# Loading TensorE's weight-address registers two at a time instead of eight at a time in a mixture-of-experts loop

## The chip, the cores and the metric

The kernel runs on one NeuronCore of a Trainium2 chip. The metric is the device time of one execution in microseconds (us), the median of several runs. The core has five engines that run side by side and wait for one another through semaphores: TensorE (PE, matrix products; its weight loads are shown apart as PEld), VectorE (DVE), ScalarE (ACT), GpSimd (POOL) and SyncE (SP), which here only starts transfers. Each engine has a sequencer that reads its instructions in order; instructions that only the sequencer handles (register arithmetic, loads into registers, semaphore waits) are shown in the profile with a q behind the engine's name.

## What is computed

The reference is one transformer layer on x of shape 4 x 1024 x 128: causal attention with 16 heads, then a mixture of 8 experts of which each token takes 2, plus a shared expert. The part that the change touches is the experts:

```python
logits = xn @ gate_w.T
probs = jax.nn.softmax(logits, axis=-1)
tk_probs, tk_idx = jax.lax.top_k(probs, TOP_K)
...
out = _swiglu(xf, sWg, sWu, sWd)
for e in range(NUM_EXPERTS):
    out = out + w[:, e:e + 1] * _swiglu(xf, Wg[e], Wu[e], Wd[e])
```

where `_swiglu(x, wg, wu, wd)` is `silu(x @ wg) * (x @ wu) @ wd`, with 128 inputs, 256 inner columns and 128 outputs.

## The kernel before

The kernel first projects and stores queries and keys, then runs attention (until about 635 us of the span), then the experts. The 8192 pairs of token and expert are sorted by expert into rows of a tensor in HBM, `sorted_rows`, and padded so that each tile of 128 rows belongs to one expert. There are `TILES` = 72 tiles, worked off as `NP` = 36 pairs; the loop variable of the pair is `q`.

Which expert a tile belongs to is known only at run time. It is written as an offset into the weights to `w_at`, one int32 for each tile, in on-chip memory. PE reads it from there into its own registers with `pe.load` (the instruction TENSOR_LOAD, line 1721, in `load_regs(a, n)`: n registers, for tiles a to a+n-1). There are `BATCH` = 24 registers, and tile k uses register k % 24. `expert_at(k)` (line 1770) turns such a register into the address that the weight operands of `tile_gate_up` and `tile_down` use. SP has 24 registers of its own for the rows of `sorted_rows` and loads them 24 at a time at line 1262, and 8 for the padding at line 1248.

The tile table comes in two parts. The first 24 offsets (`EARLY_TILES`) are loaded into registers ahead of the loop, 8 at a time. The other 48 are loaded in the loop: from `q` = `LATE_FROM` = 9 on, `AHEAD` = 3 pairs ahead of their use, behind a wait for the transfers that write the table (`tiles_in`).

One turn of the loop on PE, for pair q, holds in this order:

- `tile_gate_up(q, 0)`: three matmuls against 512 columns for the gate and up weights (lines 1786 to 1788; the operands are split in two parts so that three passes give the product),
- `turn_h(q - 1)`: four transposes of the pair before (line 1794), which wait for DVE's product `tile_h(q - 1)` (line 1587),
- `tile_gate_up(q, 1)`, then `turn_rows(q + 2)`: two transposes of the rows that come two pairs later (line 1776),
- `tile_down(q - 1)`: eight matmuls of the down projection (line 1805), which wait for DVE's copy `keep_hT(q - 1)` (line 1594),
- on some turns, `load_regs`.

Beside it ACT does `tile_silu(q)` (line 1383), `keep_hi(q + 2)` (line 1377) and `keep_y(q - 1)` (line 1391). DVE does, each turn, `destination(q)` (lines 1578 and 1581), `keep_hT(q - 1)` (line 1594), `tile_h(q)` (line 1587), pieces of the final sum and its norm from q = 23 on (a hand-written table, `PIECES`: adds at line 1433, statistics at lines 1424, 1449 and 1452), and `keep_lo(q + 2)` (line 1570). POOL scatters the results (line 1309). SP fetches rows, nine pairs deep. Each engine runs its instructions in the order in which the code writes them; no scheduler reorders them.

The profile's names for buffers are those of the memory that they reuse: `k_space` on line 1805 is the transposed hidden tile, `q_space` on line 1587 the hidden tile, `expT` the fetched rows.

Of the kernel before, what the change touches and what calls it, by code (L numbers as in the profile page):

```python
# [219 lines left out]
def block_kernel(nc, x_d, wq_d, wqs_d, bq_d, wk_d, wks_d, bk_d, wkv_d, bkv_d, wv_d, bv_d, wo_d, bo_d,  # L220
# [13 lines left out]
    with ExitStack() as top:  # L234
# [778 lines left out]
        with ExitStack() as two:  # L1013
# [149 lines left out]
            AHEAD, LATE_FROM = 3, EARLY_TILES // 2 - 3  # L1163
            B_XT, B_HT, B_Y = (0, 1), 7, 6
            NP = TILES // 2
# [516 lines left out]
            def tensor_behind(pe, item):  # L1682
# [37 lines left out]
                def load_regs(a, n):  # L1720
                    pe.load(regs[a % BATCH:a % BATCH + n], w_at[0:1, a:a + n])
# [50 lines left out]
                def turn_rows(q):  # L1772
                    pe.wait_ge(xt_in[q % TILE_RING], DMA * 2 * (q // TILE_RING + 1))
                    wait(pe, t_lo_ok, q - 1)
                    for i in range(2):
                        last = nc.tensor.transpose(ps[:, B_XT[q % 2], P * i:P * (i + 1)], xt[:, q % TILE_RING, i, 0:E], identf[:])
                    last.then_inc(xt_turned, 1)

                def tile_gate_up(q, i):
                    at = expert_at(2 * q + i)  # L1780
                    if i == 0:
                        pe.wait_ge(t_lo_ok, q + 1)
                        wait(pe, h_ok, q - 1)
                    out = ps[:, 2 + 2 * (q % 2) + i]
                    hi, lo = t_hi[:, q % 2, P * i:P * (i + 1)], t_lo[:, q % 2, P * i:P * (i + 1)]
                    nc.tensor.matmul(out, hi, wide_hi[:, bass.ds(at, 2 * INTER)], start=True, stop=False)  # L1786
                    nc.tensor.matmul(out, hi, wide_lo[:, bass.ds(at, 2 * INTER)], start=False, stop=False)  # L1787
                    nc.tensor.matmul(out, lo, wide_hi[:, bass.ds(at, 2 * INTER)], start=False, stop=True).then_inc(gu_ok, 1)  # L1788

                def turn_h(q):  # L1790
                    pe.wait_ge(h_ok, q + 1)
                    wait(pe, hT_ok, q)
                    for i in range(4):
                        last = nc.tensor.transpose(ps[:, B_HT, P * i:P * (i + 1)], hu[:, q % 2, P * i:P * (i + 1)],  # L1794
                                                   identf[:])
                    last.then_inc(h_turned, 1)

                def tile_down(q):
                    pe.wait_ge(hT_ok, q + 1)
                    wait(pe, y_kept, 2 * q)  # L1800
                    for i in range(2):
                        at = expert_at(2 * q + i)
                        out = ps[:, B_Y, P * i:P * (i + 1)]
                        for f in range(2):
                            last = nc.tensor.matmul(out, hT[:, q % 2, INTER * i + P * f:INTER * i + P * (f + 1)],  # L1805
                                                    wide_down[:, bass.ds(at + P * f, P)], start=f == 0, stop=f == 1)
                    last.then_inc(y_made, 1)
# [7 lines left out]
                for q in range(NP):  # L1815
                    tile_gate_up(q, 0)
                    if q > 0:
                        turn_h(q - 1)
                    tile_gate_up(q, 1)
                    if q + 2 < NP:  # L1820
                        turn_rows(q + 2)
                    if q > 0:
                        tile_down(q - 1)
                    if q == LATE_FROM:
                        pe.wait_ge(tiles_in, 4 * DMA)
                    if q >= LATE_FROM and (q - LATE_FROM) % 4 == 0 and q + AHEAD < NP:
                        load_regs(2 * (q + AHEAD), 8)
                turn_h(NP - 1)
                gate_up(FRONT, 0)
                tile_down(NP - 1)  # L1830
# [380 lines left out]
            def _(pe):  # L2211
# [116 lines left out]
                for s in range(NS - LAG, NS):  # L2328
                    for part in range(2):
                        product(G - 1, s, part)  # L2330
                tensor_behind(pe, item)


# [44 lines left out]
```

## Time and profile before

| what | value |
| --- | --- |
| median of 3 runs | 819.85 us (818.8 to 823.23) |
| the profiled execution's own time | 819.85 us |
| span from its first to its last instruction | 818.1 us |
| PE busy | 735.1 us, 90% of the span |
| PE weight loads busy | 352.7 us, 43% |
| DVE busy | 628.3 us, 77% |
| ACT busy | 510.6 us, 62% |
| POOL busy | 337.0 us, 41% |
| TensorE clock granted, mean | 0.96 of full speed |

The profiled execution took what the median run took; 1.75 us of it lie outside the span. The rows are read as follows. The chain of waits follows the work that ended last back to the beginning. The timeline has instructions in order of time, with the idle time of the engine just before them in brackets and what ended it. The view of one line of the code gives its instructions' durations in ns as smallest, median and largest.

### The profile page before, as it was taken

What the parts mean: (1) busy time and instruction counts of PE and PEld (TensorE: products, weight loads), DVE (VectorE), ACT (ScalarE), POOL (GpSimd) and SP (SyncE); (2) the same over time, 40 slices, a digit from 0 to 9 for tenths busy, and PEclk for the clock granted to TensorE, in tenths of its full rate; (3) what the DMA queues carried; (4) which work ended last, traced back from release to release, by engine and by line L of the source; (5) the groups of instructions that cost most, each with busy time, mean ns of one, the idle gap of its engine ahead of it and who ended that gap; (6) DMA issues with size and microseconds to landing.
All of it is one profiled execution on the core that took longest, in us unless ns stands there. A gap on an engine that the chain in (4) does not pass through costs nothing.

```text
span 818.1 us, 17480 instructions
## 1 busy us (share of the span) xinstructions
PE 735.1 (90%) x5616; PEld 352.7 (43%) x5616; DVE 628.3 (77%) x1969; ACT 510.6 (62%) x1045; POOL 337.0 (41%) x518
## 2 busy tenths in 40 slices
PE   5788689999999999989999999999998989999991
PEld 2343123333334333433433433433333867787771
DVE  5979878988886897887788688689653557656886
ACT  3655146666766778666686776677888734444553
POOL 3666221232221323215554223464336447655662
PEclk9978579999999999999999999999999999999997
DMA  6459552413614315224153241431230423435423
GB/s 164 140 153 187 137 151 49 69 29 41 105 46 73 60 36 106 48 36 87 40 101 72 64 68 27 95 69 53 67 98 31 102 83 110 134 82 153 132 92 119
DMA packets 78529, 71.79 MB, mean 88 GB/s; under 512 B 27154, under 2 KB 58547, under 8 KB 78259
## 3 DMA queue, kind: packets, MB, share of 16 engines
q1 hardware_dynamic: 69528, 59.32, 33.0%
q0 software_dynamic: 4352, 8.99, 3.5%
q10 hardware_dynamic: 4562, 2.40, 1.1%
q8 instruction: 46, 0.75, 0.4%
q14 instruction: 41, 0.34, 0.1%
HBM read 44.24 MB, written 23.94 MB: 83 GB/s over the span
## 4 chain that ended last, share of the span: by engine, by line
PE 59%; DVE 12%; issue 7%; ACT 6%; DMA 1%; POOL 1%; POOLq 0%; SPq 0%; DVEq 0%; ACTq 0%
PE ps L2292 15%; PE ps L2319 14%; PE ps L306 11%; DVE x_in L317 5%; ACT expT L2026 4%; PE ps L1805 4%; PE ps L1786 2%; PE ps L1788 2%; PE ps L1787 2%; PE ps L1794 2%; PE ps L1714 1%; PE ps L2269 1%; ACT rows L752 1%; PE ps L977 1%; PE ps L993 1%
## 5 line engine op out<-in xcount | busy, mean ns | idle before, releaser
L2026 ACT ACTIVATE expT<-ps 128x512 f32<-128x512 f32 (+1 forms) x640 | 333.0, 553 | 148.5 <-PE ps L2319 141.4
L317 DVE CUSTOM_DVE_ANT_0 x_in<-ps,mask 128x1024 bf16<-128x1024 f32 (+7 forms) x512 | 364.2, 754 | 56.9 <-PE ps L306 53.2
L2319 PE MATMUL ps<-q_space,k_space 96*128 96x512 bf16 (+3 forms) x768 | 223.2, 333 | 8.7 <-ACT expT L2026 5.1
L306 PE MATMUL ps<-k_space,q_space 96*128 96x512 bf16 (+3 forms) x768 | 196.9, 342 | 19.3 <-DVE mx L317 15.5
L2292 PE MATMUL ps<-expT,vr 128*9 128x256 f32 (+1 forms) x2560 | 178.3, 360 | 0.9 <-POOL expT L1980 0.9
L1980 POOL TENSOR_SCALAR_AFFINE_SELECT expT<-expT 128x512 f32<-128x512 f32 x128 | 79.7, 635 | 194.7 <-ACT expT L2026 194.2
L2319 PEld LDWEIGHTS ps<-q_space,k_space 96*128 96x128 bf16 x768 | 61.9, 98 | 159.9 <-ACT expT L2026 103.6
L306 PEld LDWEIGHTS ps<-k_space,q_space 96*128 96x128 bf16 x768 | 63.9, 99 | 83.2 <-DVE mx L317 48.7
L742 POOL DMA_INDIRECT sorted_rows<-rows,places x64 | 64.0, 1000 | 58.2 <-ACT expT L2026 33.8
L1309 POOL DMA_INDIRECT expert_rows<-expT,tile_to x72 | 70.0, 972 | 38.4 <-ACT expT L1391 21.0
L2292 PEld LDWEIGHTS ps<-expT,vr 128*9 128x9 f32 x2560 | 41.3, 88 | 92.2 <-issue 47.6
L1933 POOL TENSOR_SCALAR negs<-mx 128x16 bf16<-128x16 f32 x32 | 8.4, 263 | 108.2 <-DVE mx L317 96.6
L1383 ACT ACTIVATE q_space<-ps 128x512 f32<-128x512 f32 x36 | 21.5, 597 | 44.1 <-PE ps L1788 44.1
L1805 PE MATMUL ps<-w_gu,k_space 128*128 x288 | 41.4, 287 | 4.1 <-DVE k_space L1594 3.8
L317 DVE DVE_READ_ACCUMULATOR2_ANT mx<- 128x1 f32 x512 | 42.4, 83 | 0.0
L1587 DVE TENSOR_TENSOR q_space<-q_space,ps 128x512 f32<-128x512 f32 x36 | 24.7, 687 | 20.5 <-ACT q_space L1383 20.5
L1805 PEld LDWEIGHTS ps<-w_gu,k_space 128*128 128x128 f32 x288 | 34.8, 191 | 11.8 <-issue 11.8
L1786 PE MATMUL ps<-w_hi,rows_hi 128*128 x72 | 34.4, 478 | 2.3 <-DVE q_space L1587 1.3
L1594 DVE COPY k_space<-ps 128x512 f32<-128x512 f32 x36 | 24.9, 691 | 14.2 <-PE ps L1794 14.0
L1391 ACT ACTIVATE expT<-ps,expT 128x128 f32<-128x128 f32 x72 | 22.5, 364 | 20.5 <-PE ps L1805 20.5
L1788 PE MATMUL ps<-w_hi,rows_lo 128*128 x72 | 28.4, 395 | 0.0
L1787 PE MATMUL ps<-w_lo,rows_hi 128*128 x72 | 28.2, 392 | 0.0
(239 smaller groups left out, 916.2 us busy)
## 6 DMA issues: line engine op xcount, KB each, us to landing
q_space<-q_parts SPq DMA_DIRECT2D x48, 192.0 KB
expT<-sorted_rows SPq DMA_DIRECT2D x72, 65.0 KB, 1.9
k_space<-k_parts SPq DMA_DIRECT2D x32, 128.0 KB
q_parts<-parts SPq DMA_DIRECT2D x24, 128.0 KB, 2.4
k_parts<-parts SPq DMA_DIRECT2D x24, 128.0 KB, 3.0
k_space<-k_parts SPq DMA_DIRECT2D x16, 192.0 KB
v_ones<-v_st SPq DMA_DIRECT2D x8, 288.0 KB, 3.4
vr<-v_ones SPq DMA_DIRECT2D x16, 144.0 KB
```

The source lines that it names most:

```text
L306: last = nc.tensor.matmul(psw[:, at + lo:at + hi], qr[:, g % RING, hh, qi * P:(qi + 1) * P], kr[:, g % RING, hh, lo:hi], start=True, stop= ...
L317: last = nc.vector.tensor_tensor_reduce(out=unread[:, odd, col:col + width], in0=psw[:, 2 * CT * odd + col:2 * CT * odd + col + width], in ...
L742: nc.gpsimd.indirect_dma_start(out=xs_d, out_offset=bass.IndirectOffsetOnAxis(ap=pos[:, q, k, c * NT + t:c * NT + t + 1], axis=0), in_=xs[ ...
L1309: nc.gpsimd.indirect_dma_start(out=y_d, out_offset=bass.IndirectOffsetOnAxis(ap=to[:, r, i:i + 1], axis=0), in_=yt[:, r, i], in_offset=Non ...
L1786: nc.tensor.matmul(out, hi, wide_hi[:, bass.ds(at, 2 * INTER)], start=True, stop=False)
L1787: nc.tensor.matmul(out, hi, wide_lo[:, bass.ds(at, 2 * INTER)], start=False, stop=False)
L1788: nc.tensor.matmul(out, lo, wide_hi[:, bass.ds(at, 2 * INTER)], start=False, stop=True).then_inc(gu_ok, 1)
L1805: last = nc.tensor.matmul(out, hT[:, q % 2, INTER * i + P * f:INTER * i + P * (f + 1)], wide_down[:, bass.ds(at + P * f, P)], start=f == 0 ...
L1980: nc.gpsimd.affine_select(out=tile, in_=tile, compare_op=ALU.is_ge, fill=0.0, base=0, pattern=[[0, GH], [1, P]], channel_multiplier=-1).th ...
L2026: act.activation(expT[:, (NS * g + s) % PTN, hh, 0:width], ps[:, B_S + hh % 2, 0:width], ACT.Exp, scale=SCALE).then_inc(exp_ok, 1)
L2292: last = nc.tensor.matmul(ps[32 * hh:32 * hh + VW, B_O + half, at:at + n], vr[:, g % RING, kt, hh * VW:(hh + 1) * VW], expT[:, (NS * g + s ...
L2319: last = nc.tensor.matmul(ps[:, B_S + hh % 2, col:col + m], kr[:, g % RING, hh, kt * P:(kt + 1) * P], qr[:, g % RING, hh, q0:q0 + m], star ...
```

## The change

The loads of the loop are cut up. Before, on turns q = 9, 13, 17, 21, 25 and 29, one instruction loads 8 registers. After, on each turn from q = 9 to q = 32, one instruction loads 2 registers. The same 48 values go to the same 48 places in the ring of registers; those of pair q + 3 are loaded on turn q in both or, before, up to three turns earlier. The wait for `tiles_in` stays on turn 9. The loads ahead of the loop stay 3 of 8 registers.

```diff
                     if q == LATE_FROM:
                         pe.wait_ge(tiles_in, 4 * DMA)
-                    if q >= LATE_FROM and (q - LATE_FROM) % 4 == 0 and q + AHEAD < NP:
-                        load_regs(2 * (q + AHEAD), 8)
+                    if LATE_FROM <= q < NP - AHEAD:
+                        load_regs(2 * (q + AHEAD), 2)
```

The first place is on PE between turn 10 and turn 11, of the kernel before. The rows at L1805 are the end of `tile_down(9)`, those from L1786 on the start of `tile_gate_up(11, 0)`; ISA and REGISTER_ALU are the register arithmetic of the weights' address.

```order
L1770 ISA
L1805 MATMUL ps<-w_gu,k_space 128x128
L1805 ISA
L1805 MATMUL ps<-w_gu,k_space 128x128
L1786 ISA
L1786 MATMUL ps<-w_hi,rows_hi 128x512
L1787 REGISTER_ALU
L1787 MATMUL ps<-w_lo,rows_hi 128x512
L1788 MATMUL ps<-w_hi,rows_lo 128x512
```

The same place on PE in the changed kernel.

```order
L1770 ISA
L1805 MATMUL ps<-w_gu,k_space 128x128
L1805 ISA
L1805 MATMUL ps<-w_gu,k_space 128x128
L1721 TENSOR_LOAD w_at
L1786 ISA
L1786 MATMUL ps<-w_hi,rows_hi 128x512
L1787 REGISTER_ALU
L1787 MATMUL ps<-w_lo,rows_hi 128x512
L1788 MATMUL ps<-w_hi,rows_lo 128x512
```

One load has come between the last matmul of a turn and the address arithmetic of the next. It has done so at 18 turns (10 to 12, 14 to 16, 18 to 20, 22 to 24, 26 to 28, 30 to 32); at the six turns that had a load it stands where it stood. PE's program is 18 rows longer, and nothing else in it differs.

The second place is on DVE in turn 28, one of the turns with statistics. Its rows are the same in both kernels: `tile_h(28)`, the statistics of one chunk, `keep_lo(30)`, `destination(29)`, and `keep_hT(28)`, for which PE's `tile_down(28)` waits.

```order
L1587 TENSOR_TENSOR q_space<-q_space,ps 128x512
L1424 BN_STATS out_stats<-q_space 128x6 x4
L1449 BN_AGGR out_mean_var<-out_stats 128x2 x4
L1452 TENSOR_SCALAR out_var_eps<-out_mean_var 128x4
L1570 TENSOR_TENSOR rows_lo<-ps,rows_hi 128x256
L1578 SCALAR_TENSOR_TENSOR dump_rows<-expT,tab 128x2
L1581 TENSOR_TENSOR tile_to<-dump_rows,expT 128x2
L1594 COPY k_space<-ps 128x512
```

Nothing has moved on DVE, ACT, POOL or SP.

## Rows read from the trace of the kernel before

**Rows 1.** The page, chain that ended last, by engine.
```profile
PE 59%; DVE 12%; issue 7%; ACT 6%; DMA 1%; POOL 1%; POOLq 0%; SPq 0%; DVEq 0%; ACTq 0%
```

**Rows 2.** Busy time by stretch, turns 9 to 21; the columns are in the row.
```profile
core 0: us, PE busy (x) PEld busy (x) DVE busy (x) ACT busy (x) POOL busy (x), PEclk, DMA share, GB/s
...
701.12:740.49 39.37, 38.71 (x241) 31.58 (x240) 23.33 (x60) 17.98 (x49) 23.11 (x25) 1.00 0.33 91
```

**Rows 3.** Waits, 701.1 to 792 us: waiter, releaser, us in total, times, longest.
```profile
PE ps L1805 <- DVE k_space L1594: 2.9, 5, 0.8
PEld ps L1786 <- issue: 2.6, 6, 0.5
```

**Rows 4.** Timeline of PEld, first weight load of each `tile_down`: start, us [idle before].
```profile
701.12 0.97 PEld L1805 LDWEIGHTS ps<-w_gu,k_space 128*128 128x128 f32 x8 [0.19 <-issue]
704.77 0.97 PEld L1805 LDWEIGHTS ps<-w_gu,k_space 128*128 128x128 f32 x8 [0.20 <-issue]
707.92 0.97 PEld L1805 LDWEIGHTS ps<-w_gu,k_space 128*128 128x128 f32 x8 [0.19 <-issue]
...
714.25 0.97 PEld L1805 LDWEIGHTS ps<-w_gu,k_space 128*128 128x128 f32 x8 [0.19 <-issue]
717.91 0.97 PEld L1805 LDWEIGHTS ps<-w_gu,k_space 128*128 128x128 f32 x8 [0.18 <-issue]
...
727.39 0.97 PEld L1805 LDWEIGHTS ps<-w_gu,k_space 128*128 128x128 f32 x8 [0.19 <-issue]
731.01 0.97 PEld L1805 LDWEIGHTS ps<-w_gu,k_space 128*128 128x128 f32 x8 [0.19 <-issue]
...
740.49 0.97 PEld L1805 LDWEIGHTS ps<-w_gu,k_space 128*128 128x128 f32 x8 [0.20 <-issue]
744.25 0.97 PEld L1805 LDWEIGHTS ps<-w_gu,k_space 128*128 128x128 f32 x8 [0.19 <-issue]
747.41 0.97 PEld L1805 LDWEIGHTS ps<-w_gu,k_space 128*128 128x128 f32 x8 [0.18 <-issue]
750.73 0.97 PEld L1805 LDWEIGHTS ps<-w_gu,k_space 128*128 128x128 f32 x8 [0.34 <-issue]
753.89 0.97 PEld L1805 LDWEIGHTS ps<-w_gu,k_space 128*128 128x128 f32 x8 [0.19 <-issue]
757.81 0.97 PEld L1805 LDWEIGHTS ps<-w_gu,k_space 128*128 128x128 f32 x8 [0.43 <-issue]
760.97 0.97 PEld L1805 LDWEIGHTS ps<-w_gu,k_space 128*128 128x128 f32 x8 [0.19 <-issue]
764.18 0.97 PEld L1805 LDWEIGHTS ps<-w_gu,k_space 128*128 128x128 f32 x8 [0.24 <-issue]
768.05 0.97 PEld L1805 LDWEIGHTS ps<-w_gu,k_space 128*128 128x128 f32 x8 [0.91 <-issue]
771.69 0.97 PEld L1805 LDWEIGHTS ps<-w_gu,k_space 128*128 128x128 f32 x8 [0.19 <-issue]
775.49 0.97 PEld L1805 LDWEIGHTS ps<-w_gu,k_space 128*128 128x128 f32 x8 [0.83 <-issue]
778.77 0.97 PEld L1805 LDWEIGHTS ps<-w_gu,k_space 128*128 128x128 f32 x8 [0.33 <-issue]
781.94 0.97 PEld L1805 LDWEIGHTS ps<-w_gu,k_space 128*128 128x128 f32 x8 [0.19 <-issue]
```

**Rows 5.** Timeline of all engines, after turn 9's load and in turn 29.
```profile
702.50 0.19 PEld L1786 LDWEIGHTS ps<-w_hi,rows_hi 128*128 128x128 f32 x1 [0.41 <-issue]
...
768.06 1.15 PE L1805 MATMUL ps<-w_gu,k_space 128*128 x8 [0.68 <-DVE k_space L1594]
```

**Rows 6.** PE's register loads by line, whole span, then 740 to 742 us: min/median/max ns.
```profile
L1721 PEldq TENSOR_LOAD <-w_at x9: 589/595/992, 638.4 to 768.5; - x9
...
L1721 PEldq TENSOR_LOAD <-w_at x1: 667/667/667, 741.0 to 741.0; - x1
```

**Rows 7.** SP's register loads by line: 8 registers (L1248), 24 registers (L1262), ns.
```profile
L1248 SPq TENSOR_LOAD <-pad_at x1: 539/539/539, 661.7 to 661.7; - x1
...
L1262 SPq TENSOR_LOAD <-row_at x2: 1527/1534/1542, 694.1 to 728.5; - x2
```

## The prediction, made before the changed kernel was run

> **What bounds the kernel now.** I read the chain of waits first: 59% of it is PE, the next engine has 12% [rows 1]. The change touches only the expert loop's turns 9 to 32, so that stretch decides. In turns 9 to 21 PE is busy 38.71 of 39.37 us, and DVE, the next, 23.33 [rows 2]: there PE's order is the time. From turn 23 on DVE has the final sum beside its usual work, and PE now and then waits for DVE's copy, five times for 2.9 us in all [rows 3].
>
> The beat of the loop is read off the first weight load of each `tile_down` [rows 4]. The row at 701.12 is turn 9, then each row is the next turn; the third row is turn 11, 714.25 turn 13, 727.39 turn 17, and from 740.49, turn 21, every turn stands there up to 781.94, turn 33. A plain turn lasts 3.16 us (757.81 to 760.97, and 744.25 to 747.41). A turn with a load of 8 registers lasts 3.65 (turn 9), 3.66 (turn 13), 3.62 (turn 17), 3.76 (turn 21) and 3.64 (turn 29). So such a load costs 0.49, 0.50, 0.46, 0.60 and 0.48 us of PE's time. The sixth, turn 25, is read below. The same stalls show as PE's weight load at line 1786 idle with nothing to wait for, 2.6 us in 6 times [rows 3], 0.41 us in the one of turn 9 [rows 5].
>
> The load itself takes 0.59 us (0.589 smallest, 0.595 median of nine; 0.667 on turn 21) [rows 6]. It costs 0.49 and not 0.59 because the sequencer runs a little ahead of the array: the eight matmuls of `tile_down` are still being worked off when the load starts. **About 0.10 us of a load are hidden by this cover, the rest stalls PE.**
>
> **The change part by part.** It removes six loads of 8 registers and puts in 24 loads of 2. How many registers are loaded stays the same, 48. All hangs on what a load of 2 takes, and the trace of before has none on any engine.
>
> *The price of a load of 2.* The nearest rows are SP's: 8 registers took 0.539 us, 24 registers 1.534 (two of them, within 1%) [rows 7]. That is 1.534 - 0.539 = 0.995 us for 16 more registers, 0.062 each, and a straight line through both leaves 0.04 us for a load of none. So time goes nearly as the number of registers. On PE, six registers fewer make 0.59 - 6 x 0.062 = 0.22 us. The lower bound is pure proportion, 0.59 x 2/8 = 0.15; the upper one is that two cost what eight do, 0.59, since no row lies below 8 and a fixed part could hide behind it. I take 0.22, the line through the rows that exist; both ends are kept for the range.
>
> The Trainium skill speaks for either end. "DMA: Bandwidth & Descriptors", section "Latency and other measured facts", gives `tensor_load` a floor of about 600 ns, which a compiler is said to spread over four unrolled iterations. By it 24 loads would cost as much each as the six did, and the change would be the wrong way round; PE's 0.589 fits it, SP's 0.539 is a little under it. "Runtime: NRT & Kernel Launch", section "Instruction fetch mechanics", says that such loads cost about 200 ns for each register even in bulk. That is for HBM, and in size it is far from the 0.062 here, but its form is the line above. The two can't both hold for 2 registers.
>
> *The stall of a load of 2.* 0.22 less the cover of 0.10 is 0.12 us where PE is the bound. The cover is the same at every turn, since what precedes the load is the same eight matmuls.
>
> *Where the 24 loads fall.* Where PE waits for DVE anyway, a load before that wait is hidden. PEld's idle time before `tile_down` is 0.19 us on a plain turn; what it is above that is the slack that the turn before it has to give [rows 4]: 0.15 for turn 23 (row 750.73), 0.24 for turn 25 (757.81), 0.05 for turn 27 (764.18), 0.72 for turn 28 (768.05), 0.64 for turn 30 (775.49), 0.14 for turn 31 (778.77). In these turns DVE's run from `tile_h` through sum or statistics, `keep_lo` and `destination` to `keep_hT` ends last. It starts from the gate and up products of the turn's own pair, which stand ahead of that turn's load, so the load can't push it. In turn 28 PE itself sits idle 0.68 us for that copy [rows 5].
>
> Sum, in us, new stalls less old:
> - turns 9 to 20: 12 x 0.12 = 1.44, less 0.49 + 0.50 + 0.46 = 1.45: **-0.01**
> - turns 21 to 24: three at 0.12 and turn 23's within its 0.15, 0.36, less 0.60: **-0.24**
> - turns 25 to 28: turn 26 0.12, turn 27 0.12 - 0.05 = 0.07, turns 25 and 28 hidden; the old load of turn 25 gives nothing back, since its turn of 3.92 us ended with a wait for DVE that only grows if the load shrinks: **+0.19**
> - turns 29 to 32: turns 29 and 32 0.12 each, 30 and 31 hidden, 0.24, less 0.48: **-0.24**
>
> Together -0.3 us. Behind turn 32 the last pairs and the tail (scatter, fetch back, norm, store) follow from PE's last `tile_down`, so a shift of the loop reaches the end undiminished. ACT, DVE, POOL and SP issue what they issued; their rings wait for PE or are ahead of it. The wait for the second part of the table stays on turn 9 and is as early or late as before. Registers arrive at least three turns ahead of use, so nothing waits for a late load. Against the profiled execution's 819.85, which is the median too, this makes **819.5 us**.
>
> **The rivals.** *A fixed price for each load.* The 18 added loads, on PE's sequencer between `tile_down` and the next `tile_gate_up`, then stall 0.49 each in an open turn. By the same four groups: 12 x 0.49 - 1.45 = 4.43; 3 x 0.49 + 0.34 - 0.60 = 1.21; 0.49 + 0.44 = 0.93; 2 x 0.49 + 0.35 - 0.48 = 0.85; together +7.4, **827.3 us**. It is slower by more than 0.5% from the point where a load of 2 takes about 0.43 us (a stall of 0.33: 2.51 + 0.57 + 0.61 + 0.37 = 4.1). For it: there is no row below 8 registers, and a read has some latency whatever its size. Against it: 24 registers took 2.8 times what 8 took, and a fixed part big enough would have shown as an intercept, which is 0.04.
> This is also where the floor in the skill's DMA page, named above, would put the time.
>
> *A part of it fixed.* PE's load is 0.05 us longer than SP's for the same 8, so PE may have a fixed part of its own, or registers may be read in groups. With 0.40 us for a load of 2, a stall of 0.30: 2.15 + 0.45 + 0.55 + 0.28 = +3.4, **823.3 us**, still within 0.5%.
>
> *Wholly hidden.* If a load of 2 takes 0.10 to 0.15 us, the stalls are 0 to 0.05, and the old ones are gained: at 0, -1.45 - 0.60 - 0.48 = -2.5, **817.3 us**; at 0.05, -1.6, 818.2. For it: pure proportion. Against it: both engines show a little more than proportion. No further gain is to be had, as the six loads cost no more than that.
>
> **How the numbers follow.** The line through SP's rows, 0.17 to 0.27 us a load: 0.65. Partly fixed, up to 0.43: 0.11. Fixed, over 0.43: 0.15. Hidden or nearly, under 0.17: 0.09. The range takes in the hidden end and the partly fixed one and about 1 us on the outer side of each for the runs' own scatter (lowest and median of before are 1.05 apart): 816.8 to 824.5; it leaves out most of the fixed case. A measurement of this kernel can tell about 0.5%, 4.1 us, from no change. Faster by that needs more than the loads cost: 0.04, for scatter alone. Slower is the fixed case and a little of the partly fixed: 0.17. Within 0.5%: 0.79.
>
> **What would show it.** In the changed trace line 1721 has 27 loads, 24 of them short. At 0.20 to 0.25 us each the price is right; at 0.59 the rival is. Turns 10 to 12 should last 3.28 us, all alike, not 3.16 and not 3.65; turns 25, 28 and 30 should stay at 3.92, 3.87 and 3.80. PE's weight load at line 1786 should be idle a short time at 24 turns instead of 0.4 us at six. Wrong would also be a cover that differs from 0.10: since 24 loads are each reduced by it and six were, 0.05 more or less of it moves the sum by up to 1 us (19 of them are not hidden).

## The result, and the profile after

The changed kernel takes 828.0 us (median of 6 runs, 826.9 to 829.81), the kernel before 820.08 beside it (6 runs). The ratio is 1.0096, with a 95% interval of 1.0074 to 1.0118: slower by 1%, outside the range of the prediction and on the side of its first rival, which had 827.3.

The profiled execution has a span of 826.0 us, 7.9 more than before. The page still has PE at the head of the chain that ended last (before: [rows 1]).

```profile
PE 57%; DVE 13%; ACT 7%; issue 7%; POOL 1%; DMA 1%; POOLq 0%; SPq 0%; DVEq 0%; ACTq 0%
```

The view of line 1721 has the register loads: all 27 of the span, then the 13 of turns 9 to 21, then one on turn 31, as smallest, median and largest duration in ns (before: [rows 6]).

```profile
L1721 PEldq TENSOR_LOAD <-w_at x27: 536/561/1286, 638.6 to 786.8; - x27
...
L1721 PEldq TENSOR_LOAD <-w_at x13: 538/556/670, 701.8 to 745.5; - x13
...
L1721 PEldq TENSOR_LOAD <-w_at x1: 1286/1286/1286, 782.5 to 782.5; - x1
```

A load of 2 registers in the loop takes 0.56 us in the median (0.54 to 0.67 but for the one on turn 31), hardly less than the 0.59 of one with 8; the prediction had 0.22. The timeline of PEld, at the first weight load of each `tile_down` as in [rows 4], has turns 9 to 12 and the borders of the groups of turns: 701.39 is turn 9, 744.99 turn 21, 759.52 turn 25, 763.44 turn 26, 774.68 turn 29, 789.97 turn 33.

```profile
701.39 0.97 PEld L1805 LDWEIGHTS ps<-w_gu,k_space 128*128 128x128 f32 x8 [0.19 <-issue]
704.99 0.97 PEld L1805 LDWEIGHTS ps<-w_gu,k_space 128*128 128x128 f32 x8 [0.20 <-issue]
708.69 0.97 PEld L1805 LDWEIGHTS ps<-w_gu,k_space 128*128 128x128 f32 x8 [0.20 <-issue]
712.28 0.97 PEld L1805 LDWEIGHTS ps<-w_gu,k_space 128*128 128x128 f32 x8 [0.19 <-issue]
...
744.99 0.97 PEld L1805 LDWEIGHTS ps<-w_gu,k_space 128*128 128x128 f32 x8 [0.19 <-issue]
...
759.52 0.97 PEld L1805 LDWEIGHTS ps<-w_gu,k_space 128*128 128x128 f32 x8 [0.19 <-issue]
763.44 0.97 PEld L1805 LDWEIGHTS ps<-w_gu,k_space 128*128 128x128 f32 x8 [0.47 <-issue]
...
774.68 0.97 PEld L1805 LDWEIGHTS ps<-w_gu,k_space 128*128 128x128 f32 x8 [0.53 <-issue]
...
789.97 0.97 PEld L1805 LDWEIGHTS ps<-w_gu,k_space 128*128 128x128 f32 x8 [0.19 <-issue]
```

Turns 9 to 11 last 3.60, 3.70 and 3.59 us, where before one in four lasted 3.65 and the others 3.16. Set against [rows 4], group by group:

| turns | before, us | after, us | difference | prediction | fixed-price rival |
| --- | --- | --- | --- | --- | --- |
| 9 to 20 | 39.37 | 43.60 | +4.23 | -0.01 | +4.43 |
| 21 to 24 | 13.40 | 14.53 | +1.13 | -0.24 | +1.21 |
| 25 to 28 | 14.16 | 15.16 | +1.00 | +0.19 | +0.93 |
| 29 to 32 | 13.89 | 15.29 | +1.40 | -0.24 | +0.85 |

The four make 7.76 of the 7.9 us; turn 9 begins 0.27 us later, and what follows turn 32 is 0.1 to 0.2 us shorter. The waits of the loop (701.3 to 800 us; waiter, releaser, us in total, times, longest) have the stalls in one row. Where [rows 3] had 2.6 us in 6 times, it is now 10.1 in 24.

```profile
PEld ps L1786 <- issue: 10.1, 24, 1.1
```

### The profile page after: what moved, and what is told of

The parts are those of the page before. It is cut to its first block, busy times and chain, and to the rows that moved or that the text cites. A ratio compares the mean times of both kernels' runs of the same rounds, so it can differ in the third digit from the quotient of the medians.

```text
span 826.0 us, 17498 instructions
## 1 busy us (share of the span) xinstructions
PE 735.7 (89%) x5616; PEld 352.5 (43%) x5616; DVE 628.5 (76%) x1969; ACT 510.7 (62%) x1045; POOL 337.4 (41%) x518
## 4 chain that ended last, share of the span: by engine, by line
PE 57%; DVE 13%; ACT 7%; issue 7%; POOL 1%; DMA 1%; POOLq 0%; SPq 0%; DVEq 0%; ACTq 0%
PE ps L2292 15%; PE ps L2319 14%; PE ps L306 11%; DVE x_in L317 5%; ACT expT L2026 4%; PE ps L1786 3%; DVE q_space L1587 2%; PE ps L1788 2%; PE ps L1787 2%; PE ps L1805 2%; ACT q_space L1383 2%; PE ps L1794 2%; PE ps L1714 1%; PE ps L2269 1%; ACT rows L752 1%
## 5 line engine op out<-in xcount | busy, mean ns | idle before, releaser
L1805 PE MATMUL ps<-w_gu,k_space 128*128 x288 | 41.4, 287 | 3.0 <-DVE k_space L1594 2.9
L1786 PE MATMUL ps<-w_hi,rows_hi 128*128 x72 | 34.7, 482 | 6.5 <-DVE q_space L1587 4.3
L1805 PEld LDWEIGHTS ps<-w_gu,k_space 128*128 128x128 f32 x288 | 34.8, 191 | 10.6 <-issue 10.6
```

## The experiments

The chips of the experiments are slower than the one of the result (the medians of the kernel before lie between 833 and 838 us there). The loop has the same turns of 3.16 and 3.65; turn 9 begins 12 to 16 us later, at 713 to 718 us. All their profiles show the granted clock at half of full speed for 14 to 21 us between 672 and 703 us, ahead of turn 9, which the two profiles of the result don't show: the mean from 670 to 700 us is 0.77 in e1_ladder and 1.00 in the kernel before. Some of the chips scatter by several us. So each time is given as a ratio to the kernel before in the same set of runs, and what a turn or a load lasts is read from the profiles.

### Are the loads in the loop worth what the turns say?

e3_none leaves the six loads out, and with them the right weights for the tiles from 24 on.

```diff
-                    if q >= LATE_FROM and (q - LATE_FROM) % 4 == 0 and q + AHEAD < NP:
-                        load_regs(2 * (q + AHEAD), 8)
```

> The kernel before without the six loads in the loop. It leaves out their effect: the tiles from 24 on are multiplied with the weights of other experts' offsets that the registers still hold, so the output differs; the instructions and their shapes are the same. It measures what all loads in the loop cost together. By the stalls read from the turns (0.49, 0.50, 0.46, 0.60, 0.48, and turn 25's hidden) the time is 2.5 us less than before: 817.5, all plain turns at 3.16 us and turn 25 still 3.9, held by DVE. A rival: the turns with a load only gather waits that would be there without it, then less than 1 us is gained.

The timed runs fell into two groups, about 832 to 836 and 841 to 845; the ratio is 1.0008 (0.9954 to 1.0062) and doesn't settle whether 2.5 us are gained. The profile does, for the open turns: 717.54, 720.70, 723.86 are turns 9, 10 and 11, and every turn from 9 to 22 lasts 3.16 to 3.18 us. Those 14 turns take 44.31 us, and 46.25 in the profile of e1_ladder, which turned out to be the kernel before on the same chip (see below). The 1.94 us between them are what the four loads of these turns cost by the length of the turns. So the stalls come from the loads.

```profile
717.54 0.97 PEld L1805 LDWEIGHTS ps<-w_gu,k_space 128*128 128x128 f32 x8 [0.21 <-issue]
720.70 0.97 PEld L1805 LDWEIGHTS ps<-w_gu,k_space 128*128 128x128 f32 x8 [0.20 <-issue]
723.86 0.97 PEld L1805 LDWEIGHTS ps<-w_gu,k_space 128*128 128x128 f32 x8 [0.19 <-issue]
```

### Number of loads or number of registers?

e2_each8 was to have 24 loads of 8.

```diff
-                    if q >= LATE_FROM and (q - LATE_FROM) % 4 == 0 and q + AHEAD < NP:
-                        load_regs(2 * (q + AHEAD), 8)
+                    if LATE_FROM <= q < NP - AHEAD:
+                        load_regs(8 * ((q + AHEAD) // 4), 8)
```

> 24 loads at the same turns as in the changed kernel, but of 8 registers each: the aligned group of 8 that holds those of the pair three turns ahead, so most loads rewrite values that are there. If the number of loads sets the price (A), a load takes 0.59 us and not 0.55, the turns last 3.65 and the time is that of the changed kernel or up to 1 us more: 828 to 829. If the number of registers had a share of 0.06 us each beyond the fixed part (B in the loop), six more registers would cost 0.37 us at each of some 20 open turns: 835.

The built kernel has only 12 of the 24: a load whose registers are all loaded again before one of them is read is left out. What remains is two loads on neighbouring turns for each group of 8. The ratio is 1.0046 (1.0005 to 1.0088). The view of line 1721 has 15 loads with those ahead of the loop, and the first two turns with a load, 11 and 12, last 3.74 and 3.66 us.

```profile
L1721 PEldq TENSOR_LOAD <-w_at x15: 587/594/1010, 640.3 to 798.3; - x15
...
722.55 0.97 PEld L1805 LDWEIGHTS ps<-w_gu,k_space 128*128 128x128 f32 x8 [0.19 <-issue]
726.29 0.97 PEld L1805 LDWEIGHTS ps<-w_gu,k_space 128*128 128x128 f32 x8 [0.19 <-issue]
729.95 0.97 PEld L1805 LDWEIGHTS ps<-w_gu,k_space 128*128 128x128 f32 x8 [0.19 <-issue]
```

So six more loads of 8 cost about what six stalls do (6 x 0.49 = 2.9 us, 0.4%). That fits a price for each load, but also one for what a load holds. e6_four goes the other way, with 12 loads of 4.

```diff
-                    if q >= LATE_FROM and (q - LATE_FROM) % 4 == 0 and q + AHEAD < NP:
-                        load_regs(2 * (q + AHEAD), 8)
+                    if q >= LATE_FROM and (q - LATE_FROM) % 2 == 0 and q + AHEAD < NP:
+                        load_regs(2 * (q + AHEAD), 4)
```

> One part of the change: 12 loads of 4 registers, on turns 9, 11, ... 31. Theory A (the price hangs on the number of loads; 0.55 us each, 0.45 of it stall in an open turn): six more loads than before, of which those on turns 11, 15, 19, 23, 27 and 31 are new; at 0.45 and with 0.15, 0.05 and 0.14 hidden on the last three, 2.4 us, less 0.04 saved on each old one: +2.2 us, a ratio of 1.003. Theory B (the line of the prediction, 0.34 us a load of 4, 0.24 of stall): 12 x 0.24 less the old 2.5, about 0.

The ratio is 0.9991 (0.9975 to 1.0007), no difference. A load of 4 takes 0.335 us in the median, and turns 9 and 11 last 3.37 and 3.41 us, 0.21 and 0.25 more than a plain one.

```profile
L1721 PEldq TENSOR_LOAD <-w_at x15: 331/335/972, 639.2 to 790.2; - x15
...
715.03 0.97 PEld L1805 LDWEIGHTS ps<-w_gu,k_space 128*128 128x128 f32 x8 [0.19 <-issue]
718.40 0.97 PEld L1805 LDWEIGHTS ps<-w_gu,k_space 128*128 128x128 f32 x8 [0.20 <-issue]
721.55 0.97 PEld L1805 LDWEIGHTS ps<-w_gu,k_space 128*128 128x128 f32 x8 [0.19 <-issue]
```

Theory A, a fixed price for a load, falls: 4 registers cost 0.34, which is what the line of the prediction gives, and 2 registers cost 0.56. The smaller load is the dearer one.

### The price by size

e1_ladder was to measure the price by itself.

> The kernel before with loads added behind its last work: PE, behind its last matmul, loads 1, 2, 4, 8, 9, 12, 16 and 24 registers, three times each; SP does the same behind the last stores. It measures the disputed price by itself. Theory A (a fixed latency that covers up to 8 registers, then more for each further one): 1, 2, 4 and 8 registers within 0.05 us of each other at 0.53 to 0.60 us, 24 at about 1.5; 9, 12 and 16 tell whether the rise is a step for each group of 8 (9 as long as 16, about 1.0) or a slope (9 about 0.6, 16 about 1.05). Theory B (a line in the number, as the prediction took; the loop's loads of 2 were long for another reason, such as traffic in the loop): 1 register 0.1, 2 registers 0.17 to 0.22, 4 registers 0.3, 8 registers 0.55 us. PE's loads end before the last transfers, so the span changes only by SP's 24 loads at the end, some 18 us by A.

The added loads are not in the built kernel, for the reason given above, so it shows only the kernel before on that chip: turn 9 at 3.64 us, its load at 0.593. e7_sizes cuts the loads unevenly, with all values used.

```diff
-                load_regs(0, 8)
-                load_regs(8, 8)
+                load_regs(8, 16)
-                load_regs(16, 8)
+                load_regs(0, 1)
+                load_regs(1, 1)
+                load_regs(2, 2)
+                load_regs(4, 4)
...
+                SIZES = {9: (24, 12), 15: (36, 12), 21: (48, 9), 25: (57, 15)}
```

> The price by size, in loads whose registers are all used. Ahead of the loop 16 registers in one load and then 1, 1, 2 and 4; in the loop 12 on turn 9, 12 on turn 15, 9 on turn 21, 15 on turn 25, instead of six of 8. Theory A, flat up to 8: 1, 2 and 4 take 0.53 to 0.57 us each. If further registers come in groups of 8: 9, 12, 15 and 16 all take about the same, near 1.1. If they come at the 0.062 us each of SP's rows: 9 at 0.65, 12 at 0.85, 15 at 1.0, 16 at 1.1. Theory B: 1 at 0.15, 2 at 0.22, 4 at 0.34, 16 at 1.1. (A ladder of loads behind the kernel's end had been built for e1_ladder, but loads whose values nobody uses are left out when the kernel is built, so that run shows only the kernel before.)

The view of the load line, in narrow windows: 1 register, 4, 12 on turn 9, 9 on turn 21, 15 on turn 25.

```profile
L1723 PEldq TENSOR_LOAD <-w_at x1: 315/315/315, 662.5 to 662.5; - x1
...
L1723 PEldq TENSOR_LOAD <-w_at x1: 339/339/339, 664.0 to 664.0; - x1
...
L1723 PEldq TENSOR_LOAD <-w_at x1: 883/883/883, 713.9 to 713.9; - x1
...
L1723 PEldq TENSOR_LOAD <-w_at x1: 857/857/857, 753.6 to 753.6; - x1
...
L1723 PEldq TENSOR_LOAD <-w_at x1: 3717/3717/3717, 768.0 to 768.0; - x1
```

1 and 4 cost nearly the same, and 9 costs as much as the first load of 12; the second 12, on turn 15, took 1.04. The 2 between the 1 and the 4 took 0.66, the 16 took 1.29. The load of 15 seems out of any line, and its turn lasts 8.01 us; the next run explains it. The law that came out of this (law F): registers are read four at a time, what is left over one at a time, and each read takes about 0.25 us. e9_sizes2 tests it with other sizes and with starts that are not divisible by four.

```diff
+                SIZES = {9: [(24, 7)], 10: [(31, 1)], 12: [(32, 3)], 13: [(35, 5)], 14: [(40, 6)], 15: [(46, 2)],
+                         17: [(48, 4)], 18: [(52, 4)], 20: [(56, 8)], 24: [(64, 2)], 26: [(66, 4)], 27: [(70, 2)]}
...
```

> More sizes, to test a law formed from e7_sizes, e6_four and the changed kernel: 1 register 0.31 us, 2 0.54 (0.66 once), 4 0.33, 8 0.59, 9 0.86, 12 0.88, 16 1.29. Law F: registers are read four at a time, about 0.27 us a read on PE, and what is left over of a multiple of four is read one at a time at the same 0.27, with 0.05 once; so n costs 0.05 + 0.27 x (n div 4 + n mod 4). It gives 3 registers 0.86, 5 0.59, 6 0.86, 7 1.13, and 4 0.32. Ahead of the loop stand 3 (tile 0), 5 (3), 6 (8), 2 (14), 1 (16), 4 (17), 3 (21); in the loop 7 on turn 9, 1 on 10, 3 on 12, 5 on 13, 6 on 14, 2 on 15, 4 on 17 and 18, 8 on 20, 2 on 24, 4 (from 66) on 26, 2 on 27. Law G: only a start divisible by four is read in fours; then the 4 from tile 17 and the 4 from 66 take 1.13. Theory B (a line) would have 3 at 0.28, 6 at 0.47, 7 at 0.53: all below 8's 0.59.

The loads of turns 9, 10, 12, 13, 14, 15, 17 and 26, in this order: 7, 1, 3, 5 (from tile 35), 6, 2, 4 (from 48) and 4 (from 66).

```profile
L1724 PEldq TENSOR_LOAD <-w_at x1: 1092/1092/1092, 717.0 to 717.0; - x1
...
L1724 PEldq TENSOR_LOAD <-w_at x1: 308/308/308, 721.3 to 721.3; - x1
...
L1724 PEldq TENSOR_LOAD <-w_at x1: 801/801/801, 727.8 to 727.8; - x1
...
L1724 PEldq TENSOR_LOAD <-w_at x1: 1362/1362/1362, 731.6 to 731.6; - x1
...
L1724 PEldq TENSOR_LOAD <-w_at x1: 860/860/860, 736.0 to 736.0; - x1
...
L1724 PEldq TENSOR_LOAD <-w_at x1: 534/534/534, 740.0 to 740.0; - x1
...
L1724 PEldq TENSOR_LOAD <-w_at x1: 348/348/348, 746.8 to 746.8; - x1
...
L1724 PEldq TENSOR_LOAD <-w_at x1: 1014/1014/1014, 777.7 to 777.7; - x1
```

3 registers cost more than 8 did, 7 more still, as law F has it. The last two rows are both loads of 4; the one that starts at tile 66 takes three times as long. And the 5 from tile 35 cost as much as five reads, though 36 to 39 could have been one. Law G holds: only a load that starts at a place divisible by four is read in fours. Of the loads ahead of the loop, 5 from tile 3 took 1.24, 6 from tile 8 took 0.85, 2 from tile 14 took 0.55 and 1 took 0.31, as the law has them; 4 from tile 17 (1.27) and 3 from tile 21 (1.13) took 0.25 and 0.33 more than the 4 from tile 66 and the 3 from tile 32, and why is not known.

Law G also accounts for the 3.72 us in e7_sizes. Its 15 registers start at tile 57, which is not divisible by four, so they are 15 reads: at 0.25 each about 3.8 us. The turn of 8.01 us holds more than this load: behind it, from 771.90 to 775.51 us, the mean granted clock is 0.55.

### Twice the registers on the same turns

e10_four_each has the changed kernel's turns, with 4 registers on 22 of them.

```diff
-                        load_regs(2 * (q + AHEAD), 2)
+                        load_regs(2 * (q + AHEAD), 2 if (q + AHEAD) % 12 == 11 else 4)
```

> The changed kernel with 22 of its 24 loads made twice as long: 4 registers, for the next pair but three and the one behind it, where it has 2 (turns 20 and 32, where four would run past the end of the ring or the table, keep 2). Half of the loads start at a tile divisible by four. Law F: each such load is 0.33 us and not 0.54, its stall 0.24, turns 10 to 12 last 3.40, and the loop costs 22 x 0.21 = 4.6 us less than the changed kernel at most, about 4 with those that are hidden: about half way between before and the changed kernel, a ratio of 1.004 to before. Law G: every second turn is long, 1.13 us of load, and the time is above the changed kernel's. Price by the number of loads alone (A): as the changed kernel, 1.009.

It ran beside e11_after, the changed kernel itself on that chip.

> The changed kernel itself, on the same chip as e10_four_each, for the comparison with it: 1.0096 of before, turns 10 to 12 at 3.6 to 3.7 us, as in its first profile.

The ratios to the kernel before are 1.0105 (1.0039 to 1.0171) and 1.0067 (1.0033 to 1.0100); the intervals overlap, so the times alone don't order the two. In the profile of e11_after turns 10 to 12 last 3.72, 3.63 and 3.57 us, as expected, and turns 9 to 32 take 88.1 us; in that of e10_four_each these take 90.7. That profile does tell the laws apart, by turns 9 to 12 and the loads of turns 9 and 10.

```profile
715.34 0.97 PEld L1805 LDWEIGHTS ps<-w_gu,k_space 128*128 128x128 f32 x8 [0.19 <-issue]
718.70 0.97 PEld L1805 LDWEIGHTS ps<-w_gu,k_space 128*128 128x128 f32 x8 [0.20 <-issue]
723.10 0.97 PEld L1805 LDWEIGHTS ps<-w_gu,k_space 128*128 128x128 f32 x8 [0.20 <-issue]
726.47 0.97 PEld L1805 LDWEIGHTS ps<-w_gu,k_space 128*128 128x128 f32 x8 [0.19 <-issue]
...
L1721 PEldq TENSOR_LOAD <-w_at x1: 336/336/336, 715.8 to 715.8; - x1
...
L1721 PEldq TENSOR_LOAD <-w_at x1: 1242/1242/1242, 719.2 to 719.2; - x1
```

Turns 9 and 11, whose loads start at a tile divisible by four, last 3.36 and 3.37 us; turns 10 and 12 last 4.40 and 4.11. The ten loads of 4 from the other tiles take 1.01 to 1.24 us. On the odd turns twice the registers are loaded in 0.34 us, where the changed kernel needs 0.54 or more for half of them.

### The register's number or the place in memory?

In all of these the two are divisible by four together. e12_shift moves the table by two words and leaves the registers.

```diff
-            w_at = sb(two, "w_at", [1, TILES], I32)
+            w_at = sb(two, "w_at", [1, TILES + 2], I32)[:, 2:]
```

> The kernel before, with the table of weight offsets moved up by two words in its memory; the same registers are loaded by the same nine loads of 8. Both e9_sizes2 and e10_four_each bear law G out: four registers are read at once only where the load starts at a tile divisible by four, which is at once a register's number and a word's place in memory. If the place in memory decides, each load of 8 now takes eight reads, about 2.0 us instead of 0.59, and turns 9, 13 and 17 last 5.1 us. If the register's number decides, all is as before: 0.59 and 3.65 us.

The loads of 8 take 1.95 to 2.09 us, the first of the program 2.33, and turn 9 lasts 5.09, as expected if the place in memory decides. The last row is from the view of stretches, in the columns of [rows 2]; it lies in turn 17, behind its load.

```profile
L1721 PEldq TENSOR_LOAD <-w_at x9: 1952/2042/2327, 637.2 to 791.9; - x9
...
715.00 0.97 PEld L1805 LDWEIGHTS ps<-w_gu,k_space 128*128 128x128 f32 x8 [0.19 <-issue]
720.09 0.97 PEld L1805 LDWEIGHTS ps<-w_gu,k_space 128*128 128x128 f32 x8 [0.20 <-issue]
...
747.20:750.60 3.40, 3.40 (x11) 2.60 (x11) 0.69 (x1) 0.00 (x0) 1.44 (x2) 0.50 0.29 80
```

The instructions are as many as before on each engine, 17480 in all; only the table has moved by two words. So the place in memory decides. Whether the register's number must be divisible by four as well was not tried apart. The time was 846.44 us beside 833.54 for the kernel before, one execution of each; the kernel before alone scattered by 12 us on the chip of e1_ladder, so the size of the loss is better read from the turns. Turns 9, 13 and 21 last 5.09, 5.09 and 5.11 us. Six loads with 1.45 us more each make 8.7 us. Turns 17, 25 and 29 lose more than their load: turn 17 lasts 6.50 us, and behind its load the granted clock is 0.50 for 3.4 us, where it is 1.00 in turn 13. The clock is at 0.50 behind the loads of turns 25 and 29 as well.

### Can the loads be hidden?

Theory C says that a load costs PE only where its sequencer has no time to spare. Ahead of `tile_down(q - 1)` it waits for `keep_hT` anyway. e4_ahead2 and e8_ahead2b are one kernel, the changed one with its loads moved there; e5_ahead8 is the kernel before with its six loads moved.

```diff
+                    if q == LATE_FROM:
+                        pe.wait_ge(tiles_in, 4 * DMA)
+                    if LATE_FROM <= q < NP - AHEAD:
+                        load_regs(2 * (q + AHEAD), 2)
                     if q > 0:
                         tile_down(q - 1)
-                    if q == LATE_FROM:
-                        pe.wait_ge(tiles_in, 4 * DMA)
-                    if LATE_FROM <= q < NP - AHEAD:
-                        load_regs(2 * (q + AHEAD), 2)
```

> The changed kernel with its 24 loads of 2 moved, and the wait for the table with them, from behind tile_down(q - 1) to ahead of it, that is between turn_rows(q + 2) and tile_down(q - 1). There PE's sequencer stands still anyway, from its last semaphore step of the turn at 703.15 to the release of tile_down at 704.67 in the trace of before, about 1.5 us, waiting for the copy keep_hT. Theory C (a load costs only where the sequencer has no lead; the array is not disturbed): all 24 loads of 0.55 us are hidden, turns last 3.16 us, the time falls to that of no loads at all, 817 to 818. Rival D (a register load holds the sequencer and with it something else of PE wherever it stands, such as a drain of its queue): the time stays near 828.

The ratio is 0.9991 (0.9939 to 1.0044), from ten times in two groups, five at 832.65 to 833.9 and five at 841.86 to 847.86. The profiled execution is of the upper group. Its turns alternate: 715.78 is turn 9 and is followed by 4.05 us, 719.83 by 3.22, 723.05 by 3.98. In the long turn ACT's `keep_y` (line 1391) starts at 718.89, though the eight matmuls it waits for began at 715.79 and were over in 1.15 us. The first two rows show the same in turn 7, two turns before the first load of the loop (714.07 us).

```profile
708.75 1.15 PE L1805 MATMUL ps<-w_gu,k_space 128*128 x8 [0.15 <-issue]
...
711.69 0.63 ACT L1391 ACTIVATE expT<-ps,expT 128x128 f32<-128x128 f32 x2 [1.17 <-remote]
...
715.79 1.15 PE L1805 MATMUL ps<-w_gu,k_space 128*128 x8
...
718.89 0.62 ACT L1391 ACTIVATE expT<-ps,expT 128x128 f32<-128x128 f32 x2 [2.37 <-remote]
719.00 0.69 DVE L1594 COPY k_space<-ps 128x512 f32<-128x512 f32 x1 [1.44 <-PE ps L1794]
...
719.83 0.37 PE L1805 MATMUL ps<-w_gu,k_space 128*128 x1 [0.86 <-DVE k_space L1594]
```

So it was run again, with the kernel before's loads moved in the same way.

> The same kernel as e4_ahead2 once more, since its ten times there fell into two groups, about 833 and about 843 us, beside a kernel before at 834 to 838 with some at 840 to 846. Theory C: its lower group is 1 to 2.5 us below that of before, and in a profile of it turns 10 to 12 last 3.16 us. Theory E: the stalls of 0.86 us at every second turn are in this profile as well, some 10 us in all, and the time is at or above the changed kernel's.

> The kernel before with its six loads of 8 registers, and the wait for the table with them, moved ahead of tile_down(q - 1). In e4_ahead2's profile every second turn had the moved load for nothing (its tile_down began 2.27 us behind the turn's first weight load, as in a turn without a load), and every other one lost 0.86 us, since the updates of PE's semaphores from 716.95 on came in one burst at 718.86. Theory C (the moved load is hidden): turns 9, 13, 17, 21 and 29 last 3.16 us and not 3.65, 2.0 to 2.5 us less than before in all, a ratio of 0.997. Theory E (a load at that place delays the updates that keep_y and keep_hT wait for, at some of the turns): some of those five turns last 4.0, and nothing is gained.

e8_ahead2b: ratio 0.9983 (0.9973 to 0.9993), all ten times within 831.8 to 833.56. e5_ahead8: 0.9976 (0.9962 to 0.9990). The profile of e8_ahead2b, turns 9 to 12, and the load of turn 10:

```profile
713.35 0.97 PEld L1805 LDWEIGHTS ps<-w_gu,k_space 128*128 128x128 f32 x8 [0.19 <-issue]
716.51 0.97 PEld L1805 LDWEIGHTS ps<-w_gu,k_space 128*128 128x128 f32 x8 [0.20 <-issue]
719.67 0.97 PEld L1805 LDWEIGHTS ps<-w_gu,k_space 128*128 128x128 f32 x8 [0.20 <-issue]
722.83 0.97 PEld L1805 LDWEIGHTS ps<-w_gu,k_space 128*128 128x128 f32 x8 [0.20 <-issue]
...
L1721 PEldq TENSOR_LOAD <-w_at x1: 547/547/547, 715.0 to 715.0; - x1
```

The load takes what it took, 0.547 us, and the turn lasts 3.16. So theory C holds in this profile: 24 loads of 2, which cost the changed kernel 1%, are hidden by moving them over one call. In e5_ahead8, too, turns 9 to 20 last 3.15 to 3.21 us and none 3.65. Both kernels beat the kernel before, by the ratios 1.4 and 2.0 us of 834.6. Why the profiled execution of e4_ahead2 had every second turn at 4.0 us stays open. In e8_ahead2b and e5_ahead8 no such pattern is there, and in e4_ahead2 itself it starts at turn 7 (3.88 us), ahead of any moved load, so the moved loads didn't start it; whether they keep it going was not tried.

## Why the prediction was wrong

**What bounds the kernel: right.** PE's order sets the loop, and a shift of it reached the end undiminished: 7.76 us in turns 9 to 32, 7.9 in the span.

**The price of a load of 2: wrong, and this is the step that failed.** It was read off a line through 8 and 24 registers in [rows 7], and came to 0.22 us; it is 0.56 in the median. The line was right at what it was drawn through, and even at 4 (0.34 by it, 0.335 measured in e6_four). But 8 and 24 are both multiples of four: 2 and 6 reads, 0.54 and 1.53 us, which is 0.04 + 0.25 for each read. (SP's load of 24 is not as steady as the two of [rows 7] made it look: over all the profiles it took 1.17 to 1.59 us 26 times, and 0.39 and 0.45 once each.) The law by reads, with the sizes measured on PE, leaving out the first load of each program; "aligned" is a load that starts at a place of the table divisible by four:

| reads | which loads | us |
| --- | --- | --- |
| 1 | 1 register; 4 aligned | 0.31; 0.33 to 0.41, once 0.61 |
| 2 | 2 registers; 8 aligned | 0.53 to 0.56 in two of three, up to 0.74, once 1.29; 0.59 to 0.71, once 1.01 |
| 3 | 3; 6; 9; 12 | 0.80 and 1.13; 0.85 and 0.86; 0.86; 0.88 and 1.04 |
| 4 | 7; 4 not aligned | 1.09; 1.01 to 1.27 |
| 5 | 5 not aligned | 1.24 and 1.36 |
| 8 | 8 not aligned | 1.95 to 2.09 |
| 15 | 15 not aligned | 3.72 |

By it the six loads before made 12 reads and the 24 of the change make 48. The text priced proportion, the line and a constant, all of them smooth in the number. It did say, under the partly fixed rival, that registers may be read in groups, but gave that 0.40 us for 2 registers without asking what groups would mean for a load smaller than one; that two registers could cost more than four was in no candidate. The upper bound, 0.59, held the median; single loads ran above it.

**The rival had the size right by luck and the mechanism wrong.** "A fixed price for each load" gave 827.3, with its groups of turns within 0.2 us of the measured ones in three of four. But e6_four, e7_sizes and e9_sizes2 show that the price is not fixed. It is the reads that count, and a load of 2 happens to need as many as one of 8. The chance of 0.15 was too low for a case that no row excluded: the argument against it, that no intercept showed, only held if the rise was smooth between 0 and 8.

**The Trainium skill, weighed again.** The floor of about 600 ns that "DMA: Bandwidth & Descriptors" ("Latency and other measured facts") gives `tensor_load` pointed the right way here, but these loads go below it: 1 register took 0.31 us and 4 took 0.33. The other rule, about 200 ns for each register ("Runtime: NRT & Kernel Launch", "Instruction fetch mechanics"), is near what a read costs here, 0.25, wherever the registers are not read in fours. That page speaks of loads from HBM; the table here is in on-chip memory.

**The cover of 0.10 us: right on average.** The 12 loads of turns 9 to 20 take 6.94 us together, and their turns 43.60, which is 5.68 more than 12 plain ones of 3.16: 1.26 us are hidden, 0.105 a load. Single turns differ: turn 9 (load 0.549, turn 3.60) hides 0.11, turn 10 (0.543, 3.70) nothing. On turn 9 of e6_four, with 0.331 and 3.37, it is 0.12.

**Which loads are hidden by waits for DVE: mostly right.** Turns 25 and 28 last 3.92 and 3.91 us (3.92 and 3.87 before), so their loads are free, as worked out. Turn 31 is not: its load took 1.286 us and the turn 4.31 (3.28 before), 0.68 more than the rival had for it. That is more than the 0.55 us by which the group from 29 to 32 exceeds the rival. **"No further gain is to be had"** was right for shorter loads; the turns of e3_none and the ratio of e5_ahead8 bear out the 2 us or so that the old loads cost.

## What to carry to other kernels

Load registers in multiples of four from a place divisible by four, and keep the table of their values at such a place; cutting a load into pieces smaller than that makes it dearer. Put the load where the engine's sequencer waits anyway, ahead of such a wait and not behind the last matmul of a turn: the same 24 loads cost 1% at one place and nothing that could be measured at the other (e8_ahead2b). And when a price is drawn between two rows, ask what the two have in common; both of these were multiples of four.

## What the hardware showed that was not expected

- Two words of offset of a table in on-chip memory made each load of 8 registers 2.04 us instead of 0.59 (medians; e12_shift).
- Some long loads cost more than their own time. Behind the loads of turns 17, 25 and 29 of e12_shift, and behind the one of 3.72 us in e7_sizes, the granted clock is at half of full speed for about 3.4 us (0.50 in the stretch shown for turn 17; the mean is 0.55 over the 3.6 us behind the load of e7_sizes). The kernel before has its clock at 1.00 throughout turns 9 to 20. Behind turns 9, 13 and 21 of e12_shift, with loads as long, it did not fall.
- Now and then a register load takes longer than its reads: on turn 31 it was 1.286 us for 2 registers in the changed kernel, 1.010 for 8 in e2_each8 and 0.608 for 4 in e6_four, but 0.336 for 4 in e10_four_each. The first load of the program takes 0.97 to 1.00 us for 8 registers in most profiles here (0.992 in [rows 6]). An SP load runs at that time as well, but that is not all of it: in e7_sizes and e9_sizes2 the first load comes some 12 us later, without one, and takes 1.29 us for 16 registers and 0.96 for 3, about 0.25 and 0.16 above the law. The cause was not looked for.
